# A recurrent (scan) layer laid out by time step, with its key and query products beside the vector work

## Chip, cores and metric

One core of one Trainium2 chip runs the whole network as one program. The metric is device time in microseconds (us) from launch to end, median of several runs.

## What is computed

Eight sequences of 64 tokens, 512 features each (512 tokens in all), go through four layers of cross attention, attention and expert layers. The change lies in the attention slot of layer 1, which is a gated delta-rule scan with 32 heads of 32 features:

```python
xn = x * rsqrt(mean(x*x) + 1e-6) * rms_w          # on the normalised x
z, K, V = split(xn @ in_proj_W.T + in_proj_b)     # 1024, 1024 pairs, 1024
u = silu(causal_conv4(V) + conv_b)
# per token and head, from small products of u: alpha, omega, dt, sel_B (2), sel_C (2), beta, gates
A11 = (1 - a*a - w*w) / det;  A12 = 2*w / det
def step(S, (a11, a12, beta, k, v)):              # 64 steps, one pair (S0, S1) per feature
    r = (a11*S0 + a12*S1, -a12*S0 + a11*S1)
    return r + beta * (v - sum(k*r)) * k
y = sum(Q * Y);  Q = (u @ Q_W.T) * sel_C          # Y: all states
y = groupnorm(y) * silu(z) + D*u;  out = residual + y @ out_W.T
```

## The kernel before

Activations lie feature-major: a tile `[P, 8, 512]` holds 1024 features as 8 chunks of 128 partitions, and 512 tokens in the free dimension. Everything is 32-bit float. `m.ps` is the 8 PSUM banks of 512 columns. A product of one chunk of 128 output features with 512 tokens takes 4 `matmul` calls (512 input features) or 8 (1024), and each call shows as two MATMUL records. Each `m.block()` is a stretch in which the engines run their own programs and meet at its end; semaphores order them within it. `Chain` makes VectorE wait for its own last result.

`constants` (L149) is the first block. SyncE loads `x`. GpSimd makes constants, zeroes one row tile and writes it to the 12 tiles of the DRAM buffer `slot_x` (L165), which the expert layer of layer 0 fills much later, and waits for these stores; the block ends when both are done.

`L1_attn` (L2699) runs these blocks in order, with tokens as (batch, step):

- `normalise` (L189): statistics, the normalised tokens, 16 transposes, and `take`, which moves them into `m.yT`. It waits for `vectors`, all loads of this block, V's weights among them.
- `linear_features` (L277) for V, then again for the two key halves, where VectorE does the 4-tap convolution and ScalarE the silu beside it.
- `L1_coefficients` (L2788), first block: 352 small products per token (L2815) and a bias product (L2816), then a chain of some 45 short VectorE operations with ScalarE's exp, ln, sigmoid and sqrt between. Second block: transposes of the 8 quantities (L2900). Third block (L2910 to L2986): each quantity is spread from 32 head rows to 128 feature rows by a selector product over 128 rows (`head_spread`), 6 per chunk; ScalarE and VectorE take them, and VectorE and GpSimd build the 2x2 step matrix `M` (`pairs[:, 0:4]`) and the constant term (`pairs[:, 4:6]`).
- `L1_scan` (L2989): 63 steps of three chained VectorE operations over all 8 chunks (L3032, L3033, L3034). Consecutive elements of an operand lie 64 elements apart, because the step is the inner dimension. Beside it TensorE makes 12 of the 16 query products (L3017).
- `L1_readout` (L3037): two spreads per chunk (sel_C), the other 4 query products (L3071), and the sum over the pair.
- `L1_gate_and_norm` (L3092): gate products, group norm, gating.
- `linear_tokens` (L340): the output product, token-major.

## Time and profile before

| | |
|---|---|
| median of 3 runs | 3945.67 us (3939.43 to 3945.72) |
| the profiled execution | 3945.16 us |
| its span, first to last instruction | 3943.4 us |
| mean granted TensorE clock | 0.902 |
| TensorE busy | 3258.0 us, 83% of the span |
| VectorE busy | 1246.5 us, 32% |
| layer 1's scan layer | 1310.7 to 1778.1 us |

The profile gives times from the start of the span. Shares of the whole span say little about one stage: the stretches below cut the scan layer at its block ends, and each is to be read for the engine that has no idle time in it.

### The profile page before, as it was taken

The page shows a single profiled execution, that of the slowest core. Times are in us where ns is not written, and L with a number is a line of the kernel's source. Part 1 is how long each engine was busy: PE and PEld are TensorE (multiplying, and loading weights), DVE is VectorE, ACT ScalarE, POOL GpSimd, SP SyncE. Part 2 cuts the span into 40 slices and gives each one's busy share as a digit, 9 for nine tenths or more (in the row PEclk, how much of TensorE's full clock was granted, in tenths as well). Part 3 has the DMA queues.
Part 4 walks back from the last instruction along what each step waited for, and adds up shares of the span by engine and source line. Part 5 has one row for each costly group of instructions (what it writes and reads, how often), then busy time and mean ns, then how long its engine had stood idle before and what let it go on. Part 6 is the DMA issues. An engine that isn't in the chain of part 4 may idle for free. (4 is left out here: it accounts for less than half of the span.)

```text
span 3943.4 us, 41381 instructions
## 1 busy us (share of the span) xinstructions
PE 3258.0 (83%) x16625; PEld 1532.1 (39%) x16625; DVE 1246.5 (32%) x2498; ACT 676.1 (17%) x1209; POOL 152.8 (4%) x158
## 2 busy tenths in 40 slices
PE   7997789985999874987878999698999798766666
PEld 3443443432444331434334666333444473111111
DVE  2554420002444539853514131311344421000000
ACT  2432111010232120010001212011344120000000
POOL 0000010001000003000000000000000100000000
PEclk9998889997999886997988999799999899888888
DMA  3100089993110200202053120386100206999998
GB/s 128 40 29 33 27 332 406 423 427 130 43 64 22 80 22 16 86 27 96 32 205 137 41 97 1 135 346 256 43 32 11 105 38 269 420 420 420 420 420 371
DMA packets 93926, 655.37 MB, mean 166 GB/s; under 512 B 18131, under 2 KB 19028, under 8 KB 30420
## 3 DMA queue, kind: packets, MB, share of 16 engines
q1 hardware_dynamic: 89620, 639.66, 40.2%
q0 software_dynamic: 4160, 13.63, 1.0%
q8 instruction: 107, 1.75, 0.2%
q14 instruction: 39, 0.32, 0.0%
HBM read 643.75 MB, written 9.50 MB: 166 GB/s over the span
## 5 line engine op out<-in xcount | busy, mean ns | idle before, releaser
L720 PE MATMUL banks<-wvb,ctxT 128*128 128x512 f32 x768 | 346.6, 596 | 0.0
L716 PE MATMUL banks<-ctxT,wkb 128*128 128x512 f32 x512 | 230.9, 595 | 3.3 <-PEq L141 3.3
L2596 PE MATMUL banks<-ring,h 128*32 128x512 f32 x1024 | 168.6, 773 | 75.6 <-DMA ring<-in_L_ffn_w 51.7
L2584 PE MATMUL banks<-ring,mine 128*32 128x512 f32 x1024 | 161.4, 689 | 69.6 <-DMA ring<-in_L_ffn_w 68.0
L720 PEld LDWEIGHTS banks<-wvb,ctxT 128*128 128x128 f32 x768 | 139.2, 190 | 162.5 <-issue 153.6
L1574 PE MATMUL banks<-ring,xT 128*64 128x512 f32 x736 | 167.9, 610 | 12.6 <-DMA ring<-in_L_ffn_Wg 5.5
L938 DVE COPY prT<-banks 128x512 f32<-128x512 f32 x160 | 109.7, 685 | 129.8 <-PE banks L790 128.3
L2685 DVE COPY mine<-mT 128x32 f32<-128x32 f32 x31 | 5.6, 181 | 446.7 <-PE banks L2584 446.7
L491 PE MATMUL banks<-normed_features,wa 128*128 128x256 f32 x640 | 139.9, 379 | 0.7 <-ACT normed_features L457 0.7
L716 PEld LDWEIGHTS banks<-ctxT,wkb 128*128 128x128 f32 x512 | 92.7, 190 | 111.0 <-issue 99.6
L266 PE MATMUL banks<-identity,normed_tokens 128*128 128x128 f32 x144 | 39.2, 430 | 116.7 <-DVE normed_tokens L235 116.7
L838 ACT ACTIVATE pr<-pr,col 128x512 f32<-128x512 f32 x160 | 114.7, 717 | 119.4 <-DVE col L912 119.4
L491 PEld LDWEIGHTS banks<-normed_features,wa 128*128 128x128 f32 x640 | 120.7, 190 | 19.0 <-issue 2.6
L790 PE MATMUL banks<-identity,pr 128*128 128x128 f32 x640 | 105.5, 290 | 22.3 <-ACT pr L838 8.1
L716 PE MATMUL banks<-extraT,wkb 128*128 128x512 f32 x256 | 116.8, 611 | 1.0 <-ACT extraT L826 1.0
L3017 PE MATMUL banks<-u,qw 128*128 128x512 f32 x192 | 85.7, 610 | 33.5 <-DMA qw<-in_L_attn_Q_W 33.5
L790 PEld LDWEIGHTS banks<-identity,pr 128*128 128x128 f32 x640 | 77.9, 147 | 86.4 <-issue 59.7
L1574 PEld LDWEIGHTS banks<-ring,xT 128*64 128x64 f32 x736 | 62.1, 140 | 115.7 <-issue 114.5
L832 ACT ACTIVATE pr<-sc,col 128x512 f32<-128x512 f32 x96 | 69.3, 722 | 197.4 <-DVE col L907 197.4
L2596 PEld LDWEIGHTS banks<-ring,h 128*32 128x32 f32 x1024 | 28.1, 125 | 192.0 <-DMA ring<-in_L_ffn_w 139.4
L2584 PEld LDWEIGHTS banks<-ring,mine 128*32 128x32 f32 x1024 | 31.3, 115 | 177.6 <-DMA ring<-in_L_ffn_w 133.0
L308 PE MATMUL banks<-normed_features,w 128*128 128x512 f32 x192 | 92.7, 646 | 7.3 <-PEq L146 7.3
(555 smaller groups left out, 4527.4 us busy)
## 6 DMA issues: line engine op xcount, KB each, us to landing
ring<-in_L_ffn_w SPq DMA_DIRECT2D x256, 1024.0 KB, 26.8
ring<-in_L_ffn_Wd SPq DMA_DIRECT2D x24, 2048.0 KB, 25.1
ring<-in_L_ffn_Wg SPq DMA_DIRECT2D x23, 2048.0 KB, 18.2
ring<-in_L_ffn_Wu SPq DMA_DIRECT2D x23, 2048.0 KB, 19.8
wa<-in_L_ffn_W SPq DMA_DIRECT2D x32, 1024.0 KB, 13.5
wb<-in_L_ffn_W SPq DMA_DIRECT2D x32, 1024.0 KB, 11.3
ctxT<-in_ctxT SPq DMA_DIRECT2D x24, 1024.0 KB, 4.8
extra<-in_ctx SPq DMA_DIRECT2D x8, 1024.0 KB, 6.7
```

The lines of the kernel that those rows point to most:

```text
L308: ins = pe.matmul(m.ps[:, n % 4, :], buf[:, k, mm * P:(mm + 1) * P], srcT[:, k, :], start=(k == 0), stop=(k == kchunks - 1))
L491: ins = pe.matmul(m.ps[:, self.banks[q % R], 0:256], w[:, k, mm * P:(mm + 1) * P], m.yT[:, k, 256 * half:256 * half + 256], start=(k == 0) ...
L716: ins = pe.matmul(ps[:, u % 2, :], wkb[:, k, u * P:(u + 1) * P], (extraT if knorm else ctxT[:, par])[:, k, :], start=(k == 0), stop=(k == ...
L720: ins = pe.matmul(ps[:, u % 2, :], ctxT[:, par, k, r * P:(r + 1) * P], wvb[:, k, :], start=(k == 0), stop=(k == C - 1))
L790: ins = pe.transpose(ps[:, TB[j % 2], k * P:(k + 1) * P], pr[:, j % R, k * P:(k + 1) * P], m.ident[:])
L832: act.activation(pr[:, j % R, :], src, ACT.Exp, bias=col[:, par, j, 1:2], scale=1.0 if mask is not None else scale, accum_out=col[:, par, ...
L838: act.activation(pr[:, j % R, :], pr[:, j % R, :], ACT.Copy, scale=col[:, par, j, 3:4])\
L938: dve.tensor_copy(prT[:, j % RP, :, :], ps[:, TB[j % 2], :].rearrange("p (k n) -> p k n", k=KC))\
L1574: ins = pe.matmul(ps[H * side:H * side + H, 2 * kind + half, :], xT[:, p % 2, k, H * own:H * own + H], rows_of(where[(name, slot)], C)[:, ...
L2584: ins = pe.matmul(ps[B4 * q:B4 * q + B4, 0, :], mine[:, e % 2, k, :], w[:, q * 512:(q + 1) * 512], start=(k == 0), stop=(k == C - 1))
L2596: ins = pe.matmul(ps[B4 * q:B4 * q + B4, 2, :], h[:, Q * n + q, :], w[:, q * D:(q + 1) * D], start=(n == 0), stop=(n == Q - 1))
L3017: ins = pe.matmul(ps[:, n % 2 if n < NC else 2 + n - NC, :], qw[:, n % 2, k, :], u[:, k, :], start=(k == 0), stop=(k == NC - 1))
```

## The change

The scan layer becomes three blocks between `normalise` and `linear_tokens`, and tokens are now (step, batch): the 8 batch elements of a step are neighbours.

- `normalise(..., by_step=True)` writes `m.yT` in the new order; the small vectors are loaded first and V's weights last.
- `Fillers` holds 24 jobs: 8 key chunks (two products of 4 calls each) and 16 query products (8 calls each), 32 units in all, each with its weights in a ring of 4 slots, loaded as slots come free. TensorE makes a unit (`product`), ScalarE takes it from its bank (`take`).
- `L1_values`: V's products, convolution and silu chunk by chunk, and the small products accumulate over chunks in 4 banks as soon as a chunk of `u` is there. The bias product is gone; the bias is added by VectorE.
- `L1_states`: the coefficient chain, the transposes, the step matrices and the scan in one block. TensorE makes units 0 to 5 during the chain, two or one per chunk during the matrices, and 10 during the scan (29 units in all). Keys are scaled by the root of beta, so that the matrix is built from squares (on ScalarE) and one cross product. GpSimd has no part. Selectors are 32 rows high.
- `L1_outputs`: readout, the last 3 query products, the gates and the group norm in one block. Sums over steps are trees of additions in place of `tensor_reduce`. The last operation goes back to (batch, step) order.
- `constants` no longer clears `slot_x`; GpSimd does it during `L0_xattn`'s query product and waits for it in that layer's last product.

The diff, cut to its core:

```diff
 def constants(m):
...
-            step(pool.memset(m.y[:, 0, :], 0.0))
-            for p in range(SLOT_ROWS // P):
-                pool.dma_start(m.slot_x[p * P:(p + 1) * P, :], m.y[:, 0, :]).then_inc(*filled.up(16))
-            pool.wait_ge(*filled.at(SLOT_ROWS // P * 16))
...
+def normalise(m, dst, src, eps, dstT=None, scale=None, bias=None, ahead=None, vectors=None, again=None, once=None,
+              by_step=False):
...
+            out, bank = dstT[:, c, :], m.ps[:, c, :]
+            if by_step:
+                out, bank = out.rearrange("p (s b) -> p b s", b=B), bank.rearrange("p (b s) -> p b s", b=B)
...
+        def clear_slots(pool):
+            pool.memset(zero[:], 0.0).then_inc(*zeroed.up())
+            pool.wait_ge(*zeroed.at(1))
+            for p in range(SLOT_ROWS // P):
+                pool.dma_start(m.slot_x[p * P:(p + 1) * P, :], zero[:]).then_inc(*filled.up(16))
+        def slots_cleared(pool):
+            pool.wait_ge(*filled.at(SLOT_ROWS // P * 16))
...
+        vectors, out_sent = s("vectors_and_V"), s("out_weights_sent")
+        wv = qv[:, 1].rearrange("p c n -> p (c n)").rearrange("p (k n) -> p k n", k=C)
+        normalise(m, pairs[:, 0, 0:T, :], m.x, 1e-5, again=1e-6, once=m.y, dstT=m.yT, scale=rmsw[:], vectors=vectors,
+                  by_step=True, ahead=(
+                      vectors, (rmsw[:], d["L1_attn_rms_w"]), (inb[:], d["L1_attn_in_proj_b"]),
+                      (vecs[:, 0, :], d["L1_attn_conv_b"]), (vecs[:, 1, :], d["L1_attn_gn_w"]),
+                      (vecs[:, 2, :], d["L1_attn_gn_b"]), (vecs[:, 3, :], d["L1_attn_D"]), (convw[:], d["L1_attn_conv_w"]),
+                      (wv, d["L1_attn_in_V"])))
+        small = SmallParts(pairs)
+        fill = Fillers(m, ring, pairs, qv, u, inb)
+        L1_values(m, qv, u, wv, vectors, small, sel, mean, vecs, convw, inb, fill)
+        L1_states(m, pairs, u, quantT, sel, tmp, small, fill)
+        zw = pairs[:, 2].rearrange("p c n -> p (c n)").rearrange("p (k n) -> p k n", k=C)
+        L1_outputs(m, pairs, u, qv, quantT, sel, tmp, vecs, inb, mean, zw, fill, (out_sent, (pairs[:, 3], d["L1_attn_out_W"])))
+        linear_tokens(m, m.x, pairs[:, 4], None, pairs[:, 3], NC, None, m.x, sent=out_sent)
...
+class Fillers:
+    SLOTS = 4
...
+        self.jobs = [("key", c) for c in range(NC)] + [("query", n, i) for n in range(NC) for i in range(2)]
...
+    def load(self, sp):
+        f = self.loaded
+        self.loaded += 1
+        if f >= self.SLOTS:
+            last = f - self.SLOTS
+            sp.wait_ge(self.done.sem, self.done0 + self.first_unit[last] + (2 if self.jobs[last][0] == "key" else 1))
+        landed, job, d = self.landed[f % self.SLOTS], self.jobs[f], self.m.d
+        if job[0] == "key":
+            cols = slice(job[1] * P, job[1] * P + P)
+            for i in range(2):
+                sp.dma_start(self.slot(f, 8)[:, C * i:C * i + C, :], d[f"L1_attn_in_K{i}"][:, :, cols])\
+                  .then_inc(*landed.up(16))
+        else:
+            sp.dma_start(self.slot(f, 8), d["L1_attn_Q_W"][8 * job[2] + job[1]]).then_inc(*landed.up(16))
+        self.target.append(landed.made)
...
+    def product(self, pe, x):
+        f, i = self.units[x]
+        job, ps, m = self.jobs[f], self.m.ps, self.m
+        if i == 0:
+            pe.wait_ge(self.landed[f % self.SLOTS].sem, self.target[f])
+        if x >= 3:
+            pe.wait_ge(self.taken.sem, self.taken0 + x - 2)
+        bank = ps[:, 5 + x % 3, :]
+        if job[0] == "key":
+            for k in range(C):
+                ins = pe.matmul(bank, self.slot(f, 8)[:, C * i + k, :], m.yT[:, k, :], start=(k == 0), stop=(k == C - 1))
+        else:
+            for k in range(8):
+                ins = pe.matmul(bank, self.slot(f, 8)[:, k, :], self.u[:, k, :], start=(k == 0), stop=(k == 7))
+        ins.then_inc(*self.done.up())
...
+def L1_values(m, qv, u, wv, vectors, small, sel, mean, vecs, convw, inb, fill):
...
+            for _ in range(fill.SLOTS):
+                fill.load(sp)
...
+            def scalars(k):
+                if k == 0:
+                    pe.wait_ge(small_sent.sem, small_sent.made)
+                pe.wait_ge(*activated.at(k + 1))
+                for t in range(T):
+                    ins = pe.matmul(ps[:, t, 0:NS], u[:, k, t * P:(t + 1) * P], small.weights[:, k, :],
+                                    start=(k == 0), stop=(k == NC - 1))
...
+            for n in range(NC):
+                values(n)
+                if n >= 2:
+                    scalars(n - 2)
+            scalars(NC - 2)
+            scalars(NC - 1)
...
+                for back in range(1, 4):
+                    ins = dve.scalar_tensor_tensor(u[:, c, B * back:], v[:, c, :N - B * back], convw[:, c, 3 - back:4 - back],
+                                                   u[:, c, B * back:], ALU.mult, ALU.add)
...
+def L1_states(m, pairs, u, quantT, sel, tmp, small, fill):
...
+    EARLY, LATE = 6, F[8] + 13
...
+            def spread_of(bank, q, c):
+                rows = slice(H * (q % 4), H * (q % 4) + H)
+                return pe.matmul(ps[:, bank, :], sel[rows, c, :], quantT[rows, q // 4, :], start=True, stop=True)
+            def spread_keys(c):
+                if c:
+                    pe.wait_ge(*keys_used.at(c))
+                spread_of(2, 2, c)
+                spread_of(3, 3, c)
+                spread_of(4, 4, c).then_inc(*keys_spread.up())
...
+            while x < EARLY:
+                fill.product(pe, x)
+                x += 1
...
+            spread_keys(0)
+            spread_turns(0)
+            for c in range(NC):
+                more = 2 if x < F[8] else 1
+                fill.product(pe, x)
+                x += 1
+                if c + 1 < NC:
+                    spread_keys(c + 1)
+                if more == 2:
+                    fill.product(pe, x)
+                    x += 1
+                if c + 1 < NC:
+                    spread_turns(c + 1)
+            while x < LATE:
+                fill.product(pe, x)
+                x += 1
...
+            for c in range(NC):
+                act.wait_ge(*keyed.at(c + 1))
+                act.activation(squares, kappa, ACT.Square).then_inc(*squared.up())
+                for _ in range(2 if x < F[8] else 1):
+                    fill.take(act, x)
+                    x += 1
...
+            for c in range(NC):
+                dve.wait_ge(*keys_spread.at(c + 1))
+                fill.wait_taken(dve, F[c] + 1)
+                dve.tensor_tensor(kappa, ps[:, 2:4, :], state[:, :, c, :], ALU.mult).then_inc(*keyed.up())
+                dve.wait_ge(*keyed.at(c + 1))
+                dve.tensor_tensor(both, kappa[:, 0, :], kappa[:, 1, :], ALU.mult)
+                dve.tensor_tensor(value, ps[:, 4, :], u[:, c, :], ALU.mult).then_inc(*keys_used.up())
+                dve.wait_ge(*keys_used.at(c + 1))
+                dve.tensor_tensor(state[:, :, c, :], kappa, twice(value), ALU.mult)
+                dve.wait_ge(*squared.at(c + 1))
+                dve.wait_ge(*turns_spread.at(c + 1))
+                dve.scalar_tensor_tensor(M[:, 0:4:3, c, :], squares, 1.0, twice(ps[:, 0, :]), ALU.subtract, ALU.mult)
+                dve.scalar_tensor_tensor(M[:, 1:3, c, :], squares, 1.0, twice(ps[:, 1, :]), ALU.subtract, ALU.mult)
+                dve.tensor_tensor(cross, ps[:, 0:2, :], twice(both), ALU.mult).then_inc(*turns_used.up())
+                dve.wait_ge(*turns_used.at(c + 1))
+                dve.tensor_tensor(M[:, 0, c, :], cross[:, 1, :], M[:, 0, c, :], ALU.subtract)
+                dve.tensor_tensor(M[:, 2, c, :], M[:, 2, c, :], cross[:, 0, :], ALU.subtract)
+                dve.scalar_tensor_tensor(M[:, 1, c, :], M[:, 1, c, :], -1.0, cross[:, 0, :], ALU.mult, ALU.subtract)
+                ins = dve.scalar_tensor_tensor(M[:, 3, c, :], M[:, 3, c, :], -1.0, cross[:, 1, :], ALU.mult, ALU.subtract)
+            step(ins)
+            at = lambda x, n: x[:, :, :, B * n:B * n + B]
+            for n in range(1, S):
+                step(dve.tensor_tensor(
+                    terms, at(M, n).rearrange("p (i j) c b -> p i (j c) b", i=2),
+                    at(state, n - 1).rearrange("p j c b -> p (j c) b").unsqueeze(1).to_broadcast([P, 2, 2 * NC, B]), ALU.mult))
+                step(dve.tensor_tensor(r.rearrange("p (i c) b -> p i c b", i=2), terms[:, :, 0:NC, :], terms[:, :, NC:, :],
+                                       ALU.add))
+                now = at(state, n).rearrange("p j c b -> p (j c) b")
+                step(dve.tensor_tensor(now, now, r, ALU.add))
...
+def L1_outputs(m, pairs, u, qv, quantT, sel, tmp, vecs, inb, mean, zw, fill, out_load):
...
+            def outputs(c):
+                if c >= 2:
+                    pe.wait_ge(*used.at(c - 1))
+                for i in range(2):
+                    rows = slice(H * (1 + i), H * (1 + i) + H)
+                    ins = pe.matmul(ps[:, 2 * (c % 2) + i, :], sel[rows, c, :], quantT[rows, 1, :], start=True, stop=True)
...
+            outputs(0)
+            outputs(1)
+            for x in range(left, last):
+                fill.product(pe, x)
+            for c in range(2, NC):
+                outputs(c)
+                gates(c - 2)
+            gates(NC - 2)
+            for i in range(2):
+                pe.wait_ge(*summed.at(i + 1))
+                pe.matmul(ps[:, i, 0:CB], mean[:], one, start=True, stop=True).then_inc(*meaned.up())
+                if i == 0:
+                    gates(NC - 1)
...
+            pair = tmp[:, 0:2, :]
+            for c in range(NC):
+                dve.wait_ge(*spread.at(c + 1))
+                dve.tensor_tensor(pair, ps[:, 2 * (c % 2):2 * (c % 2) + 2, :], state[:, :, c, :], ALU.mult).then_inc(*used.up())
+                dve.wait_ge(*used.at(c + 1))
+                fill.wait_taken(dve, fill.first_unit[8 + 2 * c + 1])
+                step(dve.tensor_tensor(pair, pair, qv[:, :, c, :], ALU.mult))
+                step(dve.tensor_tensor(y[:, c, :], pair[:, 0, :], pair[:, 1, :], ALU.add))
...
+            def over_steps(src, chunks, signal):
+                n, src = N // 2, src[:, chunks, :]
+                part = state[:, 1, chunks, :]
+                while n >= B:
+                    o = by_chunk(one)[:, chunks, :] if n == B else part[:, :, 0:n]
+                    ins = dve.tensor_tensor(o, src[:, :, 0:n], src[:, :, n:2 * n], ALU.add)
+                    if n == B:
+                        break
+                    step(ins)
+                    src, n = part, n // 2
...
+                natural = lambda a: a.rearrange("p (s b) -> p b s", b=B)
+                dve.scalar_tensor_tensor(out[:, c, :].rearrange("p (b s) -> p b s", b=B), natural(u[:, c, :]),
+                                         vecs[:, 3, c:c + 1], natural(y[:, c, :]), ALU.mult, ALU.add)
```

`spread_turns(c)` waits for `turns_used.at(c)` and spreads quantities 0 and 1 into banks 0 and 1. `gates(n)` is one gate product of 4 calls; `gates(0)` also waits for the gate weights and for the last filler to be taken. The coefficient chain is the old one, with the bias additions (4 of 352 columns) in front, a root of beta on ScalarE, and three more products at its end.

## Rows read from the trace of the kernel before

**Rows 1.** Stretches: length, busy by engine, TensorE clock, DMA share, GB/s.

```profile
0.00:16.25 16.25, 0.00 (x0) 0.00 (x0) 0.00 (x0) 0.01 (x1) 8.31 (x22) 1.00 0.72 258
1310.70:1322.00 11.30, 4.41 (x16) 3.19 (x17) 8.25 (x20) 1.27 (x2) 2.40 (x2) 0.65 0.55 190
1322.00:1353.60 31.60, 30.58 (x64) 13.15 (x64) 3.00 (x4) 2.75 (x4) 0.00 (x0) 0.91 0.18 67
1353.60:1410.40 56.80, 55.17 (x128) 24.24 (x128) 20.92 (x32) 17.26 (x25) 0.00 (x0) 1.00 0.16 63
1410.40:1452.10 41.70, 22.90 (x72) 13.00 (x72) 14.97 (x49) 8.91 (x11) 0.00 (x0) 0.82 0.14 50
1452.10:1455.10 3.00, 1.94 (x8) 1.57 (x9) 1.38 (x2) 0.00 (x0) 0.00 (x0) 0.50 0.00 0
1455.10:1560.80 105.70, 54.30 (x96) 21.67 (x96) 95.39 (x96) 9.56 (x16) 42.65 (x16) 0.73 0.00 0
1560.80:1657.20 96.40, 85.72 (x192) 37.51 (x192) 89.48 (x189) 4.78 (x8) 0.00 (x0) 0.92 0.19 66
1657.20:1709.40 52.20, 44.72 (x96) 18.78 (x96) 26.66 (x40) 0.00 (x0) 0.00 (x0) 0.95 0.22 82
1709.40:1747.90 38.50, 29.85 (x68) 13.10 (x68) 29.89 (x32) 13.23 (x14) 0.00 (x0) 0.91 0.15 54
1747.90:1778.10 30.20, 29.24 (x64) 12.72 (x64) 5.26 (x8) 0.00 (x0) 0.00 (x0) 0.95 0.00 1
```

**Rows 2.** DMA issues, 0 to 30 us: tile, queue, count, size, us to landing.

```profile
slot_inputs<-normed_tokens POOLq DMA_DIRECT2D x12, 256.0 KB, 4.5
x_tokens<-in_x SPq DMA_DIRECT2D x1, 1024.0 KB, 5.2
```

**Rows 3.** DMA issues, 1310 to 1790 us.

```profile
qw<-in_L_attn_Q_W SPq DMA_DIRECT2D x16, 512.0 KB, 3.3
...
W<-in_L_attn_in_V SPq DMA_DIRECT2D x1, 2048.0 KB, 7.3
...
convw<-in_L_attn_conv_w SPq DMA_DIRECT2D x1, 16.0 KB, 5.8
```

**Rows 4.** Groups of instructions, 1310 to 1780 us, VectorE: busy, mean ns, idle before.

```profile
L3032 DVE TENSOR_TENSOR terms<-pairs 128x256 f32<-128x256 f32 x63 | 44.5, 707 | 2.4 <-PEq L146 0.3
...
L3034 DVE TENSOR_TENSOR pairs<-pairs,r 128x128 f32<-128x128 f32 x63 | 26.6, 422 | 2.1
...
L3033 DVE TENSOR_TENSOR r<-terms 128x128 f32<-128x128 f32 x63 | 18.4, 292 | 2.2
L2977 DVE TENSOR_TENSOR ta<-ta,tb 128x512 f32<-128x512 f32 x8 | 16.4, 2051 | 2.3 <-POOL tb L2944 2.3
...
L2979 DVE TENSOR_TENSOR tb<-ta,pairs 128x1024 f32<-128x1024 f32 x8 | 9.8, 1225 | 0.3
```

**Rows 5.** Groups of instructions, VectorE, whole span.

```profile
L1172 DVE TENSOR_TENSOR sc<-banks,edge 128x256 f32<-128x256 f32 x32 | 11.3, 417 | 2.0 <-PE banks L1006 1.6
```

**Rows 6.** Groups of instructions, 1310 to 1780 us, TensorE.

```profile
L3017 PE MATMUL banks<-u,qw 128*128 128x512 f32 x192 | 85.7, 610 | 33.5 <-DMA qw<-in_L_attn_Q_W 33.5
...
L308 PE MATMUL banks<-normed_features,pairs 128*128 128x512 f32 x128 | 55.2, 593 | 1.1 <-PEq L146 1.1
...
L2815 PE MATMUL banks<-W,u 128*128 128x352 f32 x64 | 20.0, 465 | 1.6 <-PEq L146 1.6
```

**Rows 7.** Timeline, 1531 to 1536 us: start, duration, instruction.

```profile
1531.81 1.23 DVE L2979 TENSOR_TENSOR tb<-ta,pairs 128x1024 f32<-128x1024 f32 x1
1532.95 1.22 DVE L2980 TENSOR_TENSOR tc<-ta,pairs 128x1024 f32<-128x1024 f32 x1
1534.21 0.69 DVE L2984 SCALAR_TENSOR_TENSOR pairs<-tc,pairs 128x512 f32<-128x512 f32 x1
```

**Rows 8.** Groups of instructions, 3327 to 3330 us, 32-row products.

```profile
L2572 PE MATMUL banks<-b2r,kept 32*128 32x512 f32 x8 | 2.1, 1136 | 0.0
```

**Rows 9.** Timeline, 64.9 to 66.2 us, 32-row products.

```profile
65.03 1.11 PE L746 MATMUL banks<-kT,qs 32*64 32x512 f32 x16
```

More of the change, by code:

```diff
@@ L2890, in _ @@
             dve.wait_ge(*to_dve.at(4))
[L2891 to L2904 removed]
+            tt(t0, root, sm[:, :, 6 * H:7 * H], ALU.mult)
@@ new lines, in L1_outputs @@
+def L1_outputs(m, pairs, u, qv, quantT, sel, tmp, vecs, inb, mean, zw, fill, out_load):
+    d, H, NC, CB = m.d, 32, 8, 8 * B
+    s = m.sig
+    z_sent, spread, used, step_s = s("z_weights_sent"), s("outputs_spread"), s("outputs_spread_used"), s("readout_step")
+    z_done, z_taken, centred, gated = s("z_product"), s("z_taken"), s("group_centred"), s("y_gated")
+    summed, meaned, squared, ready, rooted = s("group_summed"), s("group_mean"), s("group_squared"), s("group_var_ready"), s("group_rstd")
+    state, y, z, squares, out = pairs[:, 4:6], qv[:, 0], pairs[:, 0], pairs[:, 1], pairs[:, 4]
+    left, last = fill.first_unit[8] + 13, len(fill.units)
+    one = tmp[:, 2, 0:CB]
+    by_chunk = lambda a: a.rearrange("p (c b) -> p c b", b=B)
+    with m.block() as block:
@@ L3108, in _, with gates @@
+            def gates(n):
+                if n == 0:
+                    pe.wait_ge(z_sent.sem, z_sent.made)
+                    fill.wait_taken(pe, last - 1)
                 if n >= 4:
@@ L3124, in take_z @@
                    .then_inc(*z_taken.up())
-            take_z(0)
+            for x in range(left, last):
+                fill.take(act, x)
+            for n in range(NC - 1):
+                take_z(n)
             for half in range(2):
```

473 lines of the change are left out of this document (174 added, 299 removed).

## The prediction

> **What bounds the kernel now.** I read the page first, then the layer in stretches cut at its block ends, then the groups of instructions and single rows of the timeline. TensorE is busy 83% of the whole span, which invites the thought that only its work counts. The stretches [rows 1] say otherwise for this layer of 467.4 us (1310.7 to 1778.1). TensorE has no idle time to speak of in three of them: V (31.6), keys (56.8) and output product (30.2). The small products and their chain (41.7) are TensorE for about 23 us and then a chain of short VectorE operations. The step matrices (105.7) have VectorE busy 95.4 and GpSimd 42.7, the scan (96.4) has VectorE 89.5 of time that is all one chain. In the readout (52.2) TensorE is busy 44.7. So the layer alternates between the two engines; the 56.8 us of keys and most of the queries could lie under VectorE's time. That is what the change is to be measured by: stretch by stretch, which engine is last.
>
> **Start of the program.** The first block lasts 16.25 us, with no work but GpSimd's [rows 1]; `x` lands 5.2 us after its issue at 0.8, so at 6.0, while 12 zero stores of 256 KB go out [rows 2]. Without them the block ends about 1 us after `x`: 7.0, a gain of 9.3. The stores move under a 17 us product stretch, beside 3 MB of weight and context loads, of which the next block needs 2 MB at its start. The first stretch moved 258 GB/s at a DMA share of 0.72, so 358 while busy: 5.2 MB are 14.5 us, and I take the stores as hidden. Cover gone, they cost their own 9 at most. GpSimd's later wait lies hundreds of us after the stores.
>
> **`normalise`, 11.3 now.** V's 2 MB needed 7.3 us to land when issued second; the last small vector, issued 3.8 us into the block, landed 5.8 later, at 9.6, and the moves waited for it [rows 3]. V issued last, at about 3.4, lands at 10.7: +1.2 with the signal. The two moves per engine into the new order write each element 32 bytes from the last. The price comes from the scan: 256 elements with a stride take 0.71 us [rows 4], 256 without 0.42 [rows 5], 1.1 ns more an element; the strided 128-element addition costs 0.42 against 0.29, 1.0 ns more [rows 4]. Two moves of 512: +1.0 (bounds 0 and 1.2). 13.5.
>
> **`L1_values`.** A unit of 4 calls (8 records) costs 55.2/16 = 3.45 us at clock 1.00 [rows 6, 1]. V's 8 units are 27.6, and the stretch showed 30.6 busy at clock 0.91: 3.0 for a cold start, which stays, as the wait before it stays. The small products are 20.0 [rows 6], now between V's units; chunk k of `u` (a take, four operations of the convolution, a silu, all 512 wide, at most 0.75 each) is ready in 4.5, and 6.9 or more of TensorE's work lies before its use, so no stall. The additions of `y` to `x` lie under the first unit. 30.6 + 20.0 + 1.0 at the block's end = 51.6. The old sum for the same work was 31.6 + 56.8 (keys, gone from here) + 23.5.
>
> **`L1_states`, the chain.** The old stretch is 41.7, less 23.4 of TensorE, less 0.6 for the last copies: 17.7 [rows 1]. New: 4 additions with bias and 4 copies in front, 2.4 (352 wide, 0.53 between the 0.29 of 128 and the 0.69 of 512 [rows 4, 7]); 0.3 for the root of beta; three more products, 0.9: 21.2. Beside it 6 filler units, 6 x 3.45 = 20.7: hidden, if barely, and ScalarE's three early takes (the last at 11) are done before its next input at 14. Transposes and copies 2.8 (3.0 before, with a block's end), first spreads 1.0: VectorE starts chunk 0 at 25.0.
>
> **Step matrices.** By rows [rows 7], a 1024-wide operation that depends on nothing recent starts 1.14 after the one before it (1531.81 to 1532.95), a dependent one 1.26 (1532.95 to 1534.21); 512-wide ones by the same gaps 0.60 and 0.72. Per chunk: kappa 1.26, both 0.60, value 0.72, constant 1.14, two scaled squares 2.28, cross 1.26, four finishing operations 2.40: 9.7 us. GpSimd is out, so the 2.05 us that L2977 took where its twins take 0.69 [rows 4, 7] don't come back. Eight chunks: 77.6. The old one cost 11.9 a chunk, plus a long start. Does TensorE keep up? Two units 6.9 and five spreads. The new spreads are 32 rows high. Eight records of this very form, four row groups, took 2.1 us together with a single record at 1.14 [rows 8], and 16 records of 32x64 took 1.11 between two full-height products [rows 9]; so three spreads take about 1.0, two 0.9, and a chunk 8.8: below 9.7. One behind the other they would take 5 x 0.86 = 4.3, and TensorE's chunk would be 11.2. The rows are nearest to the first. ScalarE's square lies beside 2.5 us of VectorE work.
>
> Here a rule speaks against the change: the Trainium skill, TensorEngine Tiling (Array Packing), Key Properties, says that tiles run independently but that changing the tiling mode drains TensorE, and the new order changes it four times a chunk. The 1.11 for two passes of 0.43 puts the drain of two changes at about 0.25; with four, TensorE's chunk would be 9.3 by that rule, still below 9.7.
>
> **Scan.** The operands of a step now come in runs of 8 neighbours. 256 elements: 0.42 [rows 5] and 0.04 of gap; additions of 128: 0.29 + 0.04 each, if runs of 8 cost nothing extra. 1.115 a step against 96.4/63 = 1.53; 63 steps: 70.2. Bounds: this, and the old 96.4. I take the low end, since the strided price is one per lone element and broadcast or batched operands in runs cost nothing elsewhere (L1172's are in runs of 64). The Trainium skill, SBUF — State Buffer, Door 1, has 16-byte lines that want at least two hits each; runs of 32 bytes give four, so that rule gives 70.2 too. By it the last gating operation, which reads lone elements, is slow, as I price it below. Beside the scan TensorE has 10 queries of 6.9 (192 records in 85.7 are 7.1 each with a cold start [rows 6]), partly begun before: done about 6 early. Loads: 512 KB land in 3.3 [rows 3], wanted every 6.9 with four slots. Block: 25.0 + 77.6 + 70.2 + 0.6 = 173.4.
>
> **`L1_outputs`.** TensorE has idled, so it starts cold. It makes spreads for chunks 0 and 1, and then all three last queries before the spread of chunk 2: 2.0 + 20.7 + 2.3 (cold) + 1.0 = 26.0. VectorE needs 3.24 a chunk (1.26, 1.26, 0.72), and so stands still from 6 to 26 us. Then each chunk waits for a gate product and a spread, 4.35: chunk 7 at 47.8, its sum at 51.0. Tree over all chunks (2048, 1024, ... 64 wide) 5.4; mean 0.7; centring 4.5; two trees at 3.3, 6.6; variance, root, reciprocal, scale 2.3; scaling 4.9; gating 5.4; the last eight 0.67 each plus 512 x 1.1 ns for lone elements, 10.0. Sum 90.8, next block 0.2: 91.0, against 52.2 + 38.5 = 90.7. The merge of readout and gates gains nothing, as queries sit in front of the spreads and the trees cost more. Output product 30.2 as before; its cold start stays.
>
> **Sum.** 13.5 + 51.6 + 173.4 + 91.0 + 30.2 = 359.7 against 467.4: 107.7. With 9.3 at the start 117.0. The profiled execution took 3945.2, 0.5 below the median, so 3828.
>
> **Rivals.**
> - The scan's runs of 8 cost as much as lone elements: the old steps stay, +26.2, 3854. For it: no row shows runs of 8. Against: the rule, and runs of 61 to 64 that are free. 0.12.
> - Spreads run one after another: TensorE's chunk is 11.2, +1.5 on 7 chunks, +1.6 at the first, and +0.8 on each of 6 spreads in `L1_outputs`: +17, 3845. Against it [rows 8, 9]. 0.12.
> - Lone elements 32 bytes apart cost nothing extra (the scan's old stride was 256 bytes): -1.0 in `normalise`, -4.6 in the last gating operations, 3822. For it: no row has this stride. 0.08.
> - Slower than before, by one mechanism: ScalarE takes fillers in order with the squares, so a late filler load holds the square, and with it VectorE. The keys are loaded as pieces of 512 bytes, which no row shows. It decides once a job needs longer than the 6.9 us of its products: to lose 117 us over the 21 jobs of `L1_states` each must come 5.6 later, 512 KB per 12.5 us or 42 GB/s, where 512 KB landed in 3.3. The ring alone gives each load 20 us of slack. Over 3945: 0.02.
> - No effect, all gains given back in new waits: 0.01. Elsewhere in the sum (zero stores that delay the first layer, a wait I missed): 0.05, up to +15.
>
> The forecast keeps 0.60, with its own range 3817 to 3840. The whole range, 3812 to 3856, takes in both of the costlier cases. A measurement tells 0.2% (8 us) from no change: faster 0.97, same 0.01, slower 0.02.
>
> **What would show it.** First VectorE work at 7 us. In the scan, 63 triples 1.1 us apart (1.5: rival one). In the matrices, chunks of 9.7 us with VectorE without idle time (11 with waits for TensorE: rival two). A VectorE gap of 20 us early in `L1_outputs`, ended by a TensorE spread. Last gating operations of 1.3 us. TensorE's clock at 1.00 through `L1_states`. I am wrong if VectorE waits for ScalarE or for a filler in the chunks.

## The result, and the profile after

The changed kernel took 3820.8 us (median of 4 runs, 3819.3 to 3825.3) against 3942.6 us beside it. The ratio is 0.970, with a 95% interval of 0.969 to 0.972, so 3% faster. The forecast was 3828 with a range of 3812 to 3856: 7 us too high, well inside. The profiled execution of after took 3821.0 us with a span of 3819.2, 124.2 shorter than the span of before.

Stretches of the kernel after, cut at its block ends and at the steps of the prediction (columns as in [rows 1]):

```profile
0.00:6.10 6.10, 0.00 (x0) 0.00 (x0) 0.00 (x0) 0.02 (x1) 1.10 (x9) 1.00 0.48 172
...
16.40:35.60 19.20, 16.27 (x32) 6.88 (x32) 1.50 (x2) 1.37 (x2) 7.15 (x13) 0.98 0.86 328
1301.10:1314.50 13.40, 4.41 (x16) 3.19 (x16) 8.91 (x20) 2.10 (x2) 2.39 (x2) 0.63 0.47 160
1314.50:1363.20 48.70, 48.40 (x128) 24.89 (x128) 24.05 (x36) 11.88 (x17) 0.00 (x0) 0.96 0.35 91
1363.20:1384.00 20.80, 20.72 (x49) 9.04 (x49) 15.21 (x51) 12.17 (x17) 0.00 (x0) 1.00 0.18 52
1384.00:1387.20 3.20, 2.25 (x18) 1.55 (x18) 1.29 (x2) 0.73 (x2) 0.00 (x0) 1.00 0.52 153
1387.20:1464.50 77.30, 76.97 (x210) 29.63 (x210) 76.45 (x88) 17.12 (x21) 0.00 (x0) 1.00 0.17 55
1464.50:1535.00 70.50, 64.75 (x151) 28.31 (x149) 63.59 (x190) 5.97 (x10) 0.00 (x0) 0.99 0.18 60
1535.00:1563.10 28.10, 28.01 (x61) 11.66 (x62) 6.28 (x6) 2.31 (x4) 0.00 (x0) 0.85 0.41 168
1563.10:1589.80 26.70, 26.70 (x68) 10.13 (x69) 18.86 (x19) 4.20 (x6) 0.00 (x0) 1.00 0.00 1
1589.80:1627.90 38.10, 8.31 (x21) 3.50 (x20) 35.31 (x47) 7.31 (x7) 0.00 (x0) 0.65 0.00 0
1627.90:1658.70 30.80, 29.79 (x64) 12.86 (x64) 2.77 (x4) 0.00 (x0) 0.00 (x0) 0.93 0.00 0
```

Against [rows 1], the layer goes from 467.4 to 357.6 us. The keys' stretch of 56.8 us, in which VectorE was busy 20.9, is gone; in its place stand the step matrices (1387.2 to 1464.5), in which both engines are full. The scan is 70.5 in place of 96.4. VectorE's longest single wait lies in 1535.0 to 1563.1, where it is busy 6.28 of 28.1.

Where the 124.2 us of the two spans came from, in measured stretches: the layer 109.8, the first block 10.2 (16.3 to 6.1); layer 0's cross attention gave back 4.3 (358.0 to 362.3, the stores). The other 8.5 lie in code that the change does not touch (5.0 of them in the expert layer of layer 0, 423.4 to 418.4); on them there is more below.

VectorE's groups in the layer after; the first three are the scan (compare [rows 4]), then an operation of the matrices, the readout's first, and the last two gating operations:

```profile
L3114 DVE TENSOR_TENSOR normed_tokens<-pairs 128x256 f32<-128x256 f32 x63 | 26.8, 425 | 2.1
L3117 DVE TENSOR_TENSOR normed_tokens<-normed_tokens 128x128 f32<-128x128 f32 x63 | 18.4, 292 | 2.2
L3120 DVE TENSOR_TENSOR pairs<-pairs,normed_tokens 128x128 f32<-128x128 f32 x63 | 18.4, 292 | 2.1
L3100 DVE TENSOR_TENSOR pairs<-normed_tokens,tmp 128x1024 f32<-128x1024 f32 x8 | 9.8, 1226 | 0.3
...
L3207 DVE TENSOR_TENSOR tmp<-banks,pairs 128x1024 f32<-128x1024 f32 x8 | 9.8, 1225 | 29.5 <-PE banks L3154 29.5
...
L3255 DVE SCALAR_TENSOR_TENSOR pairs<-u,vecs,qv 128x512 f32<-128x512 f32 x8 | 8.5, 1133 | 0.0
...
L3250 DVE SCALAR_TENSOR_TENSOR qv<-qv,vecs,pairs 128x512 f32<-128x512 f32 x8 | 5.4, 747 | 0.0
```

The scan's 707, 292 and 422 ns became 425, 292 and 292. L3207 shows 29.5 us of waiting for TensorE, most of it one gap. The timeline shows that gap, 19.45 us before chunk 2, and 1.48 before each later chunk:

```profile
1540.45 1.23 DVE L3207 TENSOR_TENSOR tmp<-banks,pairs 128x1024 f32<-128x1024 f32 x1
...
1563.11 1.23 DVE L3207 TENSOR_TENSOR tmp<-banks,pairs 128x1024 f32<-128x1024 f32 x1 [19.45 <-PE banks L3154]
...
1567.80 1.22 DVE L3207 TENSOR_TENSOR tmp<-banks,pairs 128x1024 f32<-128x1024 f32 x1 [1.48 <-PE banks L3154]
```

TensorE in the matrices of after, timeline. Each line of L2957 is a set of three or of two spreads, two records a spread; each line of L2818 is one unit of four calls:

```profile
1410.36 1.13 PE L2957 MATMUL banks<-quantT,sel 32*128 32x512 f32 x6
1411.42 3.70 PE L2818 MATMUL banks<-normed_features,ring 128*128 128x512 f32 x8
1415.05 1.13 PE L2957 MATMUL banks<-quantT,sel 32*128 32x512 f32 x4
```

A set of three and a set of two cost the same, 1.06 from start to start; a unit between sets costs 3.63. A chunk is 2 x 4.69 = 9.38 us of TensorE against VectorE's 9.65 (from one chunk's first operation to the next one's).

### The profile page after: what moved, and what is told of

Same layout as the page of the kernel before. It is cut to its first block and busy times, and to the rows that moved or that the text cites. A ratio compares the mean times of both kernels' runs of the same rounds, so it can differ in the third digit from the quotient of the medians.

```text
span 3819.2 us, 41257 instructions
## 1 busy us (share of the span) xinstructions
PE 3208.4 (84%) x16601; PEld 1506.9 (39%) x16601; DVE 1203.9 (32%) x2487; ACT 681.9 (18%) x1213; POOL 110.5 (3%) x142
## 5 line engine op out<-in xcount | busy, mean ns | idle before, releaser
L2821 PE MATMUL banks<-u,ring 128*128 128x512 f32 x256 | 113.2, 603 | 0.0
## 6 DMA issues: line engine op xcount, KB each, us to landing
ring<-in_L_ffn_Wd SPq DMA_DIRECT2D x24, 2048.0 KB, 23.9
wb<-in_L_ffn_W SPq DMA_DIRECT2D x32, 1024.0 KB, 10.2
```

What stands on the lines that cost most here:

```text
L2821: ins = pe.matmul(bank, self.slot(f, 8)[:, k, :], self.u[:, k, :], start=(k == 0), stop=(k == 7))
```

## The experiments

Eleven runs edit the kernel after, one is that kernel again. The layer's own length, from the first statistics operation of its `normalise` to that of the next layer, was 357.6 or 357.7 us in all five profiles in which nothing in it was edited or where two ring slots were taken away, so shifts of half a microsecond in it can be read from one profile. Whole times wander by some 5 us around their median.

### The scan with the old strides

```diff
-            at = lambda x, n: x[:, :, :, B * n:B * n + B]
+            at = lambda x, n: x[:, :, :, n:N:S]
```

> In the 63 scan steps every operand is taken as 8 elements that lie 64 elements (256 bytes) apart, as in the old kernel, in place of 8 neighbours; number and size of the operations stay, and the scan's values are not the reference's. Theory (the scan's gain is the layout alone): the triple goes back from 1.107 to the old 1.53 us, 63 x 0.42 = 26 us more, 3847 against 3821, and the scan block's stretch 97 instead of 70.5. Rival (the step became shorter for another reason, for instance since GpSimd is gone or since the queries no longer share banks with it): the triple stays near 1.11 and the time near 3821.

3849.3 us in one run (3847 expected); the layer 381.9. Groups of VectorE in this kernel:

```profile
L3114 DVE TENSOR_TENSOR normed_tokens<-pairs 128x256 f32<-128x256 f32 x63 | 44.4, 704 | 2.2
L3120 DVE TENSOR_TENSOR pairs<-pairs,normed_tokens 128x128 f32<-128x128 f32 x63 | 26.4, 419 | 2.1
L3117 DVE TENSOR_TENSOR normed_tokens<-normed_tokens 128x128 f32<-128x128 f32 x63 | 18.4, 292 | 2.2
```

The old durations are back to 3 ns, and only in the two operations whose operands changed. The layer grew by 24.3 us: 25.7 in the scan, of which 1.4 came back behind it. The step is 1.52 us again. The theory holds, the rival is out: the gain of the scan is that neighbours in an operand are neighbours in memory.

### Each spread made twice

```diff
-                spread_of(2, 2, c)
-                spread_of(3, 3, c)
+                for bank in (2, 3, 4, 2, 3):
+                    spread_of(bank, bank, c)
                 spread_of(4, 4, c).then_inc(*keys_spread.up())
```

and the same for `spread_turns`.

> Each of the five spread products of a chunk is made twice into the same bank in the states block, the second copy signals; nothing else changes, results are the same. In the kernel after, TensorE shows 76.97 us busy of 77.3 in the step matrices and VectorE 76.45, so both are near the limit. Theory (VectorE sets the 9.65 a chunk, TensorE's own work is about 9.4 with overlap of row groups): doubled spreads add what a spread set costs, 1.0 + 0.9, to TensorE, so it becomes the bound at about 11.3 a chunk: +1.6 on 7 or 8 chunks and +1 before the first, 3833 to 3836. Rival A (spreads run one after another, 0.86 each): +4.3 a chunk, at least +30, 3851 or more. Rival B (TensorE had 2 us of slack a chunk and its busy time is only waiting): less than +3, 3821 to 3824.

3831.1 us; the layer 365.0, +7.4. TensorE's timeline:

```profile
1427.05 3.70 PE L2818 MATMUL banks<-normed_features,ring 128*128 128x512 f32 x8
1430.68 1.99 PE L2957 MATMUL banks<-quantT,sel 32*128 32x512 f32 x8
1432.60 0.70 PE L2818 MATMUL banks<-normed_features,ring 128*128 128x512 f32 x1
```

A doubled set takes 1.92 from start to start where a single one takes 1.06. So a set of two or three spreads costs 0.86, what one full-height product of 512 columns costs (3.43 for four), and 0.20 comes with going there. A unit in a row of units is 3.43, between sets 3.63: again 0.20 for going back. TensorE's chunk became 2 x 5.55 = 11.1, and VectorE's first operations of chunks 3, 4 and 5 lie 11.1 apart, as expected (11.3). The first two chunks still came at 9.65, since TensorE was ahead; the first chunk with a query in place of two key units (chunk 5) took 14.1, as the whole query stands in front of both sets. At the last chunk the kernel was 10.4 late; 3.0 of that came back behind the matrices, 1.5 of it in the stretch of the three last queries. The total is below the 3833 to 3836 that I had written, and the mechanism is the one that I had: TensorE became the bound. Rival A (spreads one behind another, +30) is out, and so is B (+3 at most). So in the kernel after TensorE had only 9.65 - 9.38 = 0.27 us of slack in a chunk.

### GpSimd at work beside the matrices

```diff
+        @block.gpsimd
+        def _(pool):
+            idle = fill.qv[:, :, NC - 1, :]
...
+            for c in range(NC):
+                pool.wait_ge(*keyed.at(c + 1))
+                for _ in range(2):
+                    beside(pool.tensor_tensor(idle, idle, idle, ALU.add))
```

> GpSimd makes two additions of 1024 elements a partition per chunk during the step matrices, on scratch of its own that nothing reads, starting when the chunk's scaled keys are there, about the load it had in the old kernel (42.7 us of GpSimd in that stretch); nothing waits for it. Theory (part of the gain is that GpSimd no longer works beside VectorE and slows it): operations of VectorE that lie beside GpSimd's become longer, as in the old kernel one took 2.05 us where its twins took 0.69, so a chunk goes from 9.65 to between 11 and 12.5: +11 to +23 over 8 chunks, 3832 to 3844. Rival (the two don't disturb each other, the old 2.05 us had another cause): chunks stay at 9.65, 3821.

3827.8 us; the layer 364.7, +7.1, chunks of 10.62 in place of 9.65. One chunk of this kernel's timeline:

```profile
1395.46 0.69 DVE L3107 TENSOR_TENSOR tmp<-normed_tokens 128x512 f32<-128x512 f32 x1
1395.57 5.17 POOL L3007 TENSOR_TENSOR qv<-qv 128x1024 f32<-128x1024 f32 x2 [5.46 <-DVE normed_tokens L3105]
1396.07 0.68 DVE L3108 TENSOR_TENSOR tmp<-banks,u 128x512 f32<-128x512 f32 x1
1396.78 2.20 DVE L3110 TENSOR_TENSOR pairs<-normed_tokens,tmp 128x1024 f32<-128x1024 f32 x1
...
1398.90 1.21 DVE L3113 SCALAR_TENSOR_TENSOR pairs<-normed_tokens,banks 128x1024 f32<-128x1024 f32 x1
1400.04 1.21 DVE L3114 SCALAR_TENSOR_TENSOR pairs<-normed_tokens,banks 128x1024 f32<-128x1024 f32 x1
```

The theory is right in kind; its size was too large (I had +11 to +23). Of the operations that start beside GpSimd's 5.17 us, one alone became longer, from 1.23 to 2.20: the one with both operands in SBUF. Those with one operand in a bank kept their time. This is what L2977 had shown [rows 4]. The Trainium skill, SBUF — State Buffer, SBUF: two separate sides, says that VectorE with two SBUF inputs and GpSimd take turns on one pair of ports, and that the later one waits for the other's whole instruction; this trace agrees, with 0.97 us more for the one operation that came second. Of the 28.4 us by which the matrices' stretch became shorter (105.7 to 77.3) GpSimd's absence is thus worth some 7; no run takes apart the rest (fewer and other operations in a chunk, the smaller spreads, the shorter way to the first chunk), which is argued from the rows alone.

### Two slots for the fillers' weights

```diff
-    SLOTS = 4
+    SLOTS = 2
```

> The ring of filler weights has two slots in place of four, so a load is issued one job (6.9 us of TensorE) before its use and not three. Theory (loads need 3.3 to 4.1 us and are never late): no change, 3821, the chunks stay at 9.65. Rival (the mechanism of my slower case: ScalarE's takes in order with the squares pass a late load on to VectorE): waits of VectorE on ScalarE's square appear in the chunks, each late microsecond of a load is one of the time; if key loads under the contention of two loads at once need 8 us, +1 a job, 3840.

3818.9 us; the layer 357.7, chunks 9.65. The loads aren't on the path; the mechanism of my slower rival isn't there even with half the ring.

### All keys before the chunks

```diff
-    EARLY, LATE = 6, F[8] + 13
+    EARLY, LATE = 16, F[8] + 13
```

> All 16 key units are made before the transposes of the coefficients, in place of 6 before and 10 between the chunks' spreads; the queries move forward, one per chunk, so that the same 29 units lie in the block. Theory (the ten units between the chunks cost nothing, as TensorE's cover there is VectorE's time): 10 x 3.45 = 34.5 us of TensorE are now uncovered, less nothing, chunks stay at 9.65: 3855. Rival (TensorE bounds the chunks as much as VectorE, so taking the key units out of them shortens nothing only because queries come in; with one query of 6.9 and spreads of 1.9 to 2.4 a chunk would be shorter if TensorE was the limit): chunks below 9.4 and the total under 3852.

3854.8 us; the layer 391.7, +34.1 against 34.5. The first scaled keys (L3095) start at 1420.1 and the last at 1487.7, 67.6 for seven chunks, the same 9.65 each as in after, though TensorE's own cycle was shorter here (8.98 from one query's start to the next one's, 1420.88 to 1429.87). So TensorE's 9.38 was not what set the 9.65: VectorE was. Ten key units under the matrices are worth 34 us, a third of the layer's whole gain.

### Queries between the spreads

```diff
-            for x in range(left, last):
-                fill.product(pe, x)
-            for c in range(2, NC):
-                outputs(c)
-                gates(c - 2)
-            gates(NC - 2)
+            for i, x in enumerate(range(left, last)):
+                fill.product(pe, x)
+                outputs(2 * i + 2)
+                outputs(2 * i + 3)
+            for n in range(NC):
+                gates(n)
+                if n in (3, 6):
```

and behind it the mean products as before.

> In the outputs block TensorE makes one of the three last queries between each two pairs of spreads, in place of all three before chunk 2's spread, and all gate products after the last spread; ScalarE's order follows. Same instructions otherwise. Theory (the 19.45 us in which VectorE stood still, and the 1.48 a chunk after it, are only the order of TensorE's queue; VectorE needs 3.2 a chunk): chunk 7's sum ends at about 37 us of the block in place of 54.7, then tree 5.4, mean, centring, trees, scaling as before, with the second mean at 55: block 76 to 78 in place of 92.9, so -15 to -17, 3804 to 3806. Rival (TensorE's total work of 54.6 us, the spreads' and gates' in it, is what sets the block's middle): the second mean and the gates are then late and the block stays above 85, -8 at most.

3805.0 us (5 runs, 3804.2 to 3812.3), ratio 0.966 [0.965, 0.968]; the kernel after itself, run beside it:

> The changed kernel itself, unchanged, beside the next ones: 3821, ratio 0.970. It gives the level for the others on the same chip.

3823.9 us (3817.1 to 3827.7), ratio 0.970 [0.969, 0.972]. The layer is 344.0 in place of 357.6: -13.6, a little short of -15. Waits of VectorE in this kernel's block, which starts at 1529:

```profile
1543.49 1.23 DVE L3208 TENSOR_TENSOR tmp<-banks,pairs 128x1024 f32<-128x1024 f32 x1 [5.57 <-PE banks L3154]
...
1567.22 0.69 DVE L3212 TENSOR_TENSOR qv<-tmp 128x512 f32<-128x512 f32 x1
...
1576.33 4.49 DVE L3235 TENSOR_TENSOR qv<-qv,banks 128x2048 f32<-128x2048 f32 x2 [3.07 <-PE banks L3179]
```

Chunk 7's sum ends at 1567.9, 38.7 into the block (37 expected, 54.7 in after). The 19.45 us are gone; gaps of 5.57, 2.53 and 2.53 are left. The edit moves the queries and the gate products at once; what each is worth alone no run shows. Then a new wait: the first mean stands behind the fourth gate product and costs 3.07. That asks for one more edit, the means behind the third and sixth gate:

> The kernel with queries between the spreads, and in addition the first mean product behind the third gate product and the second behind the sixth, in place of behind the fourth and the seventh; ScalarE's order follows. In the kernel before this edit VectorE waited 3.07 us for the first mean, which stood behind a gate product in TensorE's queue, and 0.53 for the second. Theory (that wait is only the queue's order): the first wait shrinks to about 0.8, the layer goes from 344.0 to 341.8, the median from 3805 to 3803. Rival (the gates come later and the gating waits for them): the layer stays at 344 or gets longer.

The layer is 341.2 (-2.8, and the wait 0.53). The whole, 3808.2 us (3804.0 to 3813.6), does not show it; 3803 was expected.

### The stores of zeros

Timeline of the kernel after around the end of the first product block, and DMA issues in that stretch:

```profile
32.72 0.75 DVE L324 TENSOR_SCALAR qT<-banks,b 128x512 f32<-128x512 f32 x1 [6.12 <-PE banks L306]
35.66 0.33 SPq L667 DMA_DIRECT2D ctxT<-in_ctxT  x1
35.70 0.42 ACT L817 ACTIVATE qs<-qT 128x256 f32<-128x256 f32 x1 [5.73 <-PEq L141]
35.87 12.49 PE L719 MATMUL banks<-ctxT,wkb 128*128 128x512 f32 x22 [3.19 <-PEq L141]
...
42.39 0.69 ACT L822 ACTIVATE kT<-banks,b 128x512 f32<-128x512 f32 x1 [6.27 <-PE banks L719]
```

```profile
slot_inputs<-zero POOLq DMA_DIRECT2D x12, 256.0 KB, 10.6
```

The next block starts 2.2 us after VectorE's last operation ends, where before it was 0.7, and its first product is taken 6.5 us after its start (3.7 before). Two edits ask why. One issues the stores from SyncE, in the same block behind its loads:

```diff
-                pool.dma_start(m.slot_x[p * P:(p + 1) * P, :], zero[:]).then_inc(*filled.up(16))
+                sp.dma_start(m.slot_x[p * P:(p + 1) * P, :], zero[:]).then_inc(*filled.up(16))
```

> The 12 stores of zeros stay in the first layer's query product stretch, but SyncE issues them, behind that stretch's loads, in place of GpSimd. GpSimd still makes the zero row and waits for them in the layer's last block. Theory (the block's end waits for stores that GpSimd issued, as the engine drains its own queue): the cross attention starts 0.7 us after the last VectorE operation of the stretch although the stores are still under way, and its first products take about 3.7 us: -4.3, 3817. Rival A (the end of a block waits for any engine's stores): start 2.2 us after, 3821 as before. Rival B (the stores' traffic delays the loads of the cross attention, whoever issues them): start early, but TensorE waits for its weights, 3821 or more.

The other leaves them with GpSimd and moves them to `L0_attn`:

```diff
-                        ahead=(v_sent, (w3[:], d["L0_attn_w_v"])))
+                        ahead=(v_sent, (w3[:], d["L0_attn_w_v"])), on_pool=clear_slots)
```

> The 12 stores of zeros are issued in the next layer's query and key product stretch (8 products, about 28 us) in place of the first layer's query product (4 products), and awaited in the attention block behind it. Theory (the block that issues them can't end before they have landed, and its own work was too short for them): the first layer's cross attention starts 0.7 us after the last VectorE operation in place of 2.2, TensorE hasn't stood still so long and its first products take 3.7 us in place of 6.5; -4.3, 3816 to 3817, and the new place shows no gap. Rival (what made the cross attention start slowly is not the stores but the timing of its own loads): no change within 1 us there, and 3821.

Timeline with SyncE's stores:

```profile
32.58 0.75 DVE L326 TENSOR_SCALAR qT<-banks,b 128x512 f32<-128x512 f32 x1 [6.12 <-PE banks L308]
33.99 0.33 SPq L669 DMA_DIRECT2D ctxT<-in_ctxT  x1
...
37.91 0.69 ACT L824 ACTIVATE kT<-banks,b 128x512 f32<-128x512 f32 x1 [3.46 <-PE banks L721]
```

Timeline with the stores one layer later:

```profile
30.35 0.75 DVE L324 TENSOR_SCALAR qT<-banks,b 128x512 f32<-128x512 f32 x1 [6.12 <-PE banks L306]
31.76 0.33 SPq L667 DMA_DIRECT2D ctxT<-in_ctxT  x1
...
35.67 0.69 ACT L822 ACTIVATE kT<-banks,b 128x512 f32<-128x512 f32 x1 [3.46 <-PE banks L719]
```

With SyncE's stores, as long under way (10.6 us each), the block ends 0.66 after the last operation, and the first product of the next one is taken 3.7 us after its start. With GpSimd's, the next block began at 35.6 to 35.9 in all nine kernels that have them there, though VectorE's last operation ended anywhere from 31.0 to 33.5. Three views show what lies between: GpSimd's DRAIN at the block's end in after (L146: shortest, median and longest in ns, then first and last start), two stretches of after, and one of the kernel with SyncE's stores (columns as in [rows 1]):

```profile
L146 POOLq DRAIN  x2: 34/6606/13177, 21.9 to 35.6; - x2
34.20:35.60 1.40, 0.00 (x0) 0.00 (x0) 0.00 (x0) 0.00 (x0) 0.00 (x0) 0.68 0.00 0
35.80:41.40 5.60, 5.53 (x7) 2.46 (x8) 0.00 (x0) 0.31 (x1) 0.00 (x0) 0.50 0.83 309
```

```profile
33.50:34.00 0.50, 0.00 (x0) 0.00 (x0) 0.00 (x0) 0.00 (x0) 0.00 (x0) 1.00 1.09 418
```

At the end of a block each engine executes a DRAIN. VectorE's and ScalarE's here last as long as their last operation (0.79 us for one of 0.75, 0.72 for one of 0.69). GpSimd issued its last store by 23.9 (17.2 and 6.66 us of issuing), but its DRAIN lasted 13.18 us, from 21.9 to 35.0, about 1 us beyond the end of the transfers at 34.1. So it was not the issuing that held the block. SyncE's stores were still moving at 418 GB/s when their block ended (33.5 to 34.0; all loads had landed). So the end of a block waits for stores that GpSimd issued, and not for those of SyncE; rivals A and B are out.

What slows the next block is TensorE's clock: in after it is granted 0.50 of full speed (1.2 of 2.4 GHz) from 35.8 to 41.4. TensorE had stood still for 3.2 to 5.6 us in the nine kernels with GpSimd's stores there, and in eight of them the clock fell to 0.50 before the first product was taken; in the ninth (GpSimd beside the matrices, 3.33 us) the clock stayed at 1.00 and the first product was taken after 3.7 us. In the five kernels without them (before, SyncE's stores and the three with later stores) it had stood still for 1.65 and the clock stayed at 1.00.

Two more kernels combine the edits:

> Both edits, queries between the spreads and stores of zeros one layer later. They lie 1500 us apart and should add: -16 and -4.3, so 3800 to 3802, ratio to the kernel before 0.965. Rival (a gain early in the program is lost at later cold starts): only one of the two shows, 3804 or more.

> The same, and the stores of zeros one layer later. It settles what moving the stores is worth in the whole: the first cross-attention layer was 353 to 354 us with the stores moved and 359 to 362 without in single profiles, but the two medians so far differ by -4.4 in one pair and +1.5 in the other, and in the one pair the expert layer of layer 0 was 7 us longer in the profile. Theory A (the gain stays, the expert layer's wander is chance): 5 to 7 us below the run without, 3796 to 3798. Theory B (the expert layer takes it back, through where TensorE's clock changes level): the same as the run without, within 2 us, and the expert layer's stretch 424 us in the profile.

| kernel | layer 0's cross attention | its expert layer | scan layer | median us, ratio [95%] |
|---|---|---|---|---|
| after, again | 361.2 | 417.9 | 357.6 | 3823.9, 0.970 [0.969, 0.972] |
| stores later | 354.4 | 424.7 | 357.7 | 3819.5, 0.969 [0.968, 0.971] |
| queries between | 360.1 | 416.6 | 344.0 | 3805.0, 0.966 [0.965, 0.968] |
| both | 353.0 | 417.5 | 344.3 | 3806.5, 0.966 [0.965, 0.968] |
| means earlier | 362.4 | 418.2 | 341.2 | 3808.2, 0.967 [0.965, 0.969] |
| means and stores | 357.7 | 420.2 | 341.3 | 3803.0, 0.965 [0.964, 0.967] |
| stores by SyncE (one run) | 358.1 | 426.4 | 357.6 | 3828.0 |

In the stage itself the later stores are worth 4.7 to 7.1 us in each pair: most where the first products were done early (31.0), since GpSimd's stores hold the block's end all the same. The attention layer that takes them in doesn't grow for it (114.5 to 115.3 us with them, 114.8 to 115.2 without). In the whole, the means of the three pairs differ by -4.8, -0.1 and -5.2, together -3.4 with a standard error of 1.5: a gain is likely, its size isn't settled. The levels that I had written (3800 to 3802 for both edits, 3796 to 3798 for means and stores, 3817 for SyncE's stores) were all missed by 4 us or more: the first lies where its rival had it (3804 or more), the last came with an expert layer 8 us longer than in after. The expert layer of layer 0 is 416.6 to 420.2 us in eleven profiles and 423 to 426 in three: the kernel before, the one with later stores and the one with SyncE's. Its second 30 us in after, and in the kernel with later stores, show what differs:

```profile
524.14:554.14 30.00, 27.51 (x85) 10.96 (x87) 5.49 (x27) 2.98 (x5) 9.55 (x11) 0.91 0.61 227
```

```profile
515.52:545.52 30.00, 20.27 (x52) 8.06 (x52) 5.04 (x26) 1.79 (x3) 9.58 (x11) 0.77 0.53 205
```

TensorE's granted clock (0.91 and 0.77), and with it what it got done, differs in code that is the same. In the combined kernels the same stage with moved stores is 417.5 and 420.2, so theory B of the last run (the expert layer always takes it back) falls. What decides which of the two a run gets, I did not find.

## Why the prediction was right, step by step

- **Start of the program.** First work at 6.1 (7.0 forecast). Gain 10.2 in place of 9.3.
- **The step that failed: "I take the stores as hidden".** It was wrong twice. Its 5.2 MB leave out one of the three loads that share the stretch: with it they are 6.3 MB, at its own 358 GB/s 17.6 us, longer than the 17 of the stretch; measured, the transfers ran from 17.3 to 34.1. And I asked only whether the traffic fits, not who waits for it: GpSimd's DRAIN lasts until its stores are done, so the block ended 2 us late, TensorE had stood still for 3.19 us in place of 1.65, and the next block's first products ran at half the clock. Cost 4.3 by the stage in one profile, 6 on the mean of the profiles without and with moved stores. I had 0 here, and 9 as the bound.
- **`normalise`** 13.4 (13.5). The two strided moves took 2.1 us on each engine, and they started when V's weights landed, at 1312.15.
- **`L1_values`** 48.7 (51.6). The cold start cost 1.9, not 3.0, a group of small products between V's units 2.37, not 2.5, and the block's end 0.3, not 1.0.
- **Chain and first spreads:** VectorE's first chunk at 24.0 (25.0), with quantities ready at 20.7 (21.2; the terms named there add up to 21.3). The clock was 1.00 here and in the matrices, 0.99 in the scan, as forecast.
- **Step matrices:** 9.65 a chunk (9.7), VectorE without a wait. TensorE's chunk was mis-sized: 9.38, not 8.8. The term was hidden here, by 0.27 us. The trace agrees with the rule weighed in the prediction, the Trainium skill, TensorEngine Tiling (Array Packing), Key Properties, that changing the tiling mode drains TensorE: by it the sum was 9.3. That 9.3 is so near is partly luck: two changes of the tile's height cost 0.40 where I had put 0.25, and the two sets 1.72 where I had 1.9. Rival two (spreads one behind another) is out by the second experiment.
- **Scan:** 1.11 a step (1.115), 70.0 (70.2). Rival one is out, by the trace and by the first experiment. The rule on 16-byte lines that the prediction took from the Trainium skill, SBUF — State Buffer, Door 1, gave the same; the trace agrees, with 425 ns for 256 elements in runs of 32 bytes against 417 in runs of 256 bytes [rows 5].
- **`L1_outputs`** 92.9 (91.0). The gap of 20 us is there, 19.45. The same mis-sized term is not hidden here: 4.69 a chunk in place of 4.35, +1.7. The four first spreads took 3.8 us with a cold start, where I had 2.0. Against that, the last gating operations cost 1.06 each in place of 1.25: elements 32 bytes apart cost 0.75 ns extra (1133 ns against 747 for 512 elements in L3250), not the 1.1 of the scan's 256 bytes. Rival three (nothing extra) is out.
- **Output product** 30.8 (30.2).
- **Elsewhere.** The layer was 2.1 below its forecast and the first block 0.9, the stores 4.3 above; the missing rest to 7 us is the 8.5 of unchanged stages in the profile. These are no merit of the change that I could show, since the same kernel's five repeats spread over 10 us. The terms of the change itself came to 115.7 us where I had 117.0; that they agree this well has luck in it too, as the stores' 4.3 were offset by 3.0 of small gains that I had not seen.

## What to carry to other kernels

Cut a stage into stretches and ask in each which engine has no idle time: work of the other engine that depends on nothing there (34 us of key products here) is free under it until its own cycle reaches the bound, and the queue's order decides the rest (13.6 us came from putting three queries and the gates elsewhere in TensorE's queue). Lay out a recurrent loop so that one step's elements are neighbours. When transfers are moved under other work, ask who issued them and what waits for that queue, not only whether the bytes fit.

## What the runs showed of the hardware that I had not expected

- A block's end waits for stores issued by GpSimd (its DRAIN lasted 13.18 us; next block at 35.6 to 35.9 us, whatever the products did), not for those of SyncE.
- Small products in two or three different groups of 32 rows take together 0.86 us, what one full-height product takes; a change between full-height and 32-row products costs 0.20 each way.
- VectorE's extra price for a lone element was not one number: 1.0 to 1.1 ns at 256 bytes, 0.75 ns at 32 bytes (another operation, both inputs strided), nothing in runs of 32 bytes.
- Of VectorE's operations beside GpSimd's only the one with both inputs in SBUF became longer: 1.23 to 2.20 us.
- TensorE's start after a pause follows the granted clock, and the pause alone does not fix it. In the cross attention's first block the first result took 3.7 us after a pause of 1.65 us (five kernels, clock 1.00) and 5.2 to 6.5 after pauses of 3.2 to 5.6 (eight kernels, clock 0.50 for part of it), but 3.7 after 3.33 in one (clock 1.00). The program's first product block, behind the same pause of 1.03 us, took 3.7 in six profiles and 5.4 to 6.1 in the other eight; what decides that stays open.
